# Attention and convolution on one core: the prob x val matmuls of two key chunks together in the odd units

## What is computed

```python
q = q.reshape(B * NUM_HEADS, S, hd)          # likewise k and v; hd = 64
scores = jnp.einsum('gqd,gkd->gqk', q, k) / jnp.sqrt(jnp.asarray(hd, x.dtype))
attn = jax.nn.softmax(scores, axis=-1)
wv = jnp.einsum('gqk,gkd->gqd', attn, v)
...
x = x + _L0_conv_ref(_gn(x), ...)            # _gn: group normalisation, 32 groups
x = x + _L1_conv_ref(_gn(x), ...)            # mask, relu, 3x3 convolution, bias
```

## Time and profile before

| | us |
|---|---|
| runs | 3023.82, 3025.37, 3029.92 |
| median | 3025.37 |
| span of the profiled execution | 3023.4 |
| TensorE busy | 2859.1 (95%) |
| VectorE busy | 2052.7 (68%) |
| ScalarE busy | 1035.4 (34%) |
| GpSimd busy | 897.1 (30%) |
| weigh matmuls (line 535), busy | 545.7 |
| mean granted TensorE clock | 0.983 |

### The profile page before, as it was taken

One profiled execution on the slowest core, in us unless ns is written; L12 is line 12 of the kernel. 1 busy time (PEld: TensorE's weight loads), 2 busy tenths in 40 slices (PEclk: granted clock), 3 DMA queues, 4 the chain that ended last, 5 costly groups with the idle time before them and its releaser, 6 DMA issues.

```text
span 3023.4 us, 41433 instructions
## 1 busy us (share of the span) xinstructions
PE 2859.1 (95%) x12480; PEld 1074.3 (36%) x12480; DVE 2052.7 (68%) x3010; ACT 1035.4 (34%) x1613; POOL 897.1 (30%) x619
## 2 busy tenths in 40 slices
PE   5999999999999999999999999778999999999999
PEld 2333333333333333333333333223444444444444
DVE  6786787687777777768778678987765554654521
ACT  3444444444435434434444344432121121111200
POOL 2343443443434433434343435441110010110100
PEclk9999999999999999999999999989999999999999
DMA  4303313212132142140231231121100101001000
GB/s 131 85 15 78 89 29 81 71 47 78 30 88 60 33 106 57 33 106 24 66 89 33 78 85 32 67 77 56 56 21 35 56 0 55 21 35 56 0 28 28
DMA packets 119928, 167.30 MB, mean 55 GB/s; under 512 B 27296, under 2 KB 76576, under 8 KB 119712
## 3 DMA queue, kind: packets, MB, share of 16 engines
q1 hardware_dynamic: 119712, 164.74, 19.2%
HBM read 80.16 MB, written 33.82 MB: 38 GB/s over the span
## 4 chain that ended last, share of the span: by engine, by line
PE 76%; DVE 11%; issue 5%; DMA 4%; SPq 2%; ACT 1%; DVEq 0%; POOL 0%; ACTq 0%; POOLq 0%
PE bank L625 30%; PE bank L535 11%; PE bank L523 11%; PE bank L480 10%; PE bank L498 6%; PE bank L490 4%; DVE nmax L920 2%; DVE prob_sum L914 2%; DMA den_col<-den_sb 2%; PE bank L512 2%; SPq L337 1%; DVE xn_lo L899 1%; DMA q_b<-shift 1%; DVE filt L962 1%; PE bank L506 1%
## 5 line engine op out<-in xcount | busy, mean ns | idle before, releaser
L625 PE MATMUL bank<-v_hi,filt 128*128 128x512 f16 x3072 | 920.4, 380 | 16.8 <-DVE v_lo L1178 8.7
L674 ACT ACTIVATE prob<-bank 128x512 f32<-128x512 f32 x1024 | 554.9, 593 | 818.5 <-PE bank L523 786.5
L920 DVE TENSOR_REDUCE nmax<-bank 128x1 f32<-128x512 f32 x1024 | 659.0, 682 | 188.7 <-PE bank L498 181.3
L807 POOL TENSOR_TENSOR prob_sum<-prob_sum,prob 128x512 f32<-128x512 f32 x384 | 519.7, 1353 | 730.7 <-ACT prob L674 730.2
L625 PE MATMUL bank<-v_lo,filt 128*128 128x512 f16 x1536 | 584.7, 381 | 0.0
L535 PE MATMUL bank<-prob,val 128*64 128x512 f32 x2048 | 545.7, 621 | 2.1 <-ACT prob L674 2.1
L625 PEld LDWEIGHTS bank<-v_hi,filt 128*128 128x128 f16 x3072 | 302.8, 99 | 383.4 <-issue 23.0
L498 PE MATMUL bank<-k_a,q_a 128*128 128x512 f16 x1024 | 397.6, 389 | 26.0 <-DVE nmax L920 19.7
L914 DVE TENSOR_TENSOR prob_sum<-prob_sum,prob 128x512 f32<-128x512 f32 x384 | 369.1, 961 | 20.9 <-DVE shift L930 19.6
L480 PE MATMUL bank<-mix_mem,w_mem 128*128 128x512 f16 x1024 | 331.7, 387 | 19.4 <-DVE xn_lo L899 19.4
L523 PE MATMUL bank<-q_a,k_a 128*128 128x512 f16 x1024 | 311.1, 385 | 20.6 <-ACT prob L674 20.6
(11 more groups left out here) (97 smaller groups left out, 2468.5 us busy)
## 6 DMA issues: line engine op xcount, KB each, us to landing
xr<-x SPq DMA_DIRECT2D x16, 1024.0 KB, 8.6
k_a<-pad_mem SPq DMA_DIRECT2D x64, 256.0 KB, 5.3
q_a<-pad_mem SPq DMA_DIRECT2D x64, 256.0 KB, 4.8
den_sb<-recip_scratch SPq DMA_DIRECT2D x128, 128.0 KB, 2.8
x_scratch<-xr SPq DMA_DIRECT2D x16, 1024.0 KB, 4.7
xs<-x SPq DMA_DIRECT2D x7, 2048.0 KB, 13.0
k_b<-pad_mem SPq DMA_DIRECT2D x32, 256.0 KB, 5.4
q_b<-pad_mem SPq DMA_DIRECT2D x32, 256.0 KB, 4.9
```

Of the source, the lines that this page charges most:

```text
L625: mm = pe.matmul(bank[co][:].rearrange("p (h w) -> p h w", w=PAIR), u[:, pos, ky, c, co * P:(co + 1) * P], v[:, pos, c, ky:ky + HW, :], st ...
L674: act.activation(prob[:, (2 * u + e) % 8], sc_bank[bank_turn(s * 16 + 2 * u + e, 16 * HPI)[0]][:], ACT.Exp, scale=float(D) ** -0.5).then_i ...
L807: nc.gpsimd.tensor_tensor(acc, in0, prob[:, (2 * kc + 1) % 8], ALU.add).then_inc(s1["sum1"], 1)
L920: dve.tensor_reduce(nmax[:, m // 2, m % 2:m % 2 + 1], src[:], AX.X, ALU.max, negate=True)\
```

## The change

TensorE calls `weigh` for two chunks at a time, in the odd units alone: unit 3 weighs chunks 0 and 1, unit 5 chunks 2 and 3, unit 7 chunks 4 and 5, and unit 1 of the next slot chunks 6 and 7. The matmuls, their operands and the order of the chunks are the same. In unit 1 the denominator's matmuls, which stand in place d, are directly ahead of the pair. ScalarE's copy of pv_bank moves from the end of unit 0 to unit 1, behind its two exps and ahead of that unit's q/k copies.

```diff
+            def weigh_pair(h, s, n):
+
+                weigh(h, s, 2 * n)
+                weigh(h, s, 2 * n + 1)
+
...
-                    if u == 0 and prev:
-                        weigh(h - 1, (s - 1) % HPI, SEG - 1)
-                    if u == 2:
-                        weigh(h, s, 0)
-                    if u >= 2:
-                        weigh(h, s, u - 1)
+                    if u == 1 and prev:
+                        weigh_pair(h - 1, (s - 1) % HPI, SEG // 2 - 1)
+                    if u >= 3 and u % 2:
+                        weigh_pair(h, s, u // 2 - 1)
...
-            weigh(B * HPI - 1, HPI - 1, SEG - 1)
+            weigh_pair(B * HPI - 1, HPI - 1, SEG // 2 - 1)
...
-                    if u == 0 and prev:
+                    if u == 1 and prev:
                         evacuate_pv(h - 1)
```

## The result

The changed kernel takes **3072.96 us** (median of four runs, 3070.17 to 3079.02), the kernel before 3024.6 us beside it (3018.17 to 3029.92). The ratio is 1.0163, with a 95% interval from 1.0145 to 1.0182: it is slower by 48 us. The forecast was 3030 us, 3010 to 3044.

The account below looks back on a forecast made before the run. TensorE bounds four of eight slots, VectorE partly slots 3, 4 and 7, something else slot 1. Switching saved against added waits and a later load sums to +0.7 us an image, +5 us: 3030 us, range 3010 to 3044.

Parts of the forecast that it names:

- The groups and their price: Weigh groups fall from eight to four a slot, each costing 0.24 us of switching: 0.97 us a slot saved.
- three sized waits: PE's added waits: shift matmul for nmin 0.30 us, unit 0 to 1 for an exp 0.30, unit 3 behind ScalarE's copy 0.50.
- without: Slot 5 without the later denominators' load: +0.15 us, against +0.85 with it.
- the later load is paid in full: Slot 5: the denominators' load starts 0.86 us later, PE has no slack, so the slot pays 0.86 us.
- neither moves, and everything that PE saves up to unit 5 is absorbed: Slot 1: the x load and ScalarE's 4.87 us gap stay put, so savings ahead vanish; slot total +0.1 us.
- slot 6: -0.97 + 0.30 + 0.30: Slot 6: switching saved less waits for the first exp and at the shift matmul, -0.35 us.
- slot 7, VectorE again: 0: Slot 7 follows VectorE's pace, so the change brings no difference there: 0 us.
- the hand-made replay: Slot 3 replayed with lighter units: nmin comes some 0.6 us sooner, between -0.5 and +1.0.
- VectorE's stretches "-0.15": Slots 2 and 3: +0.4 us up to slot 3's shift row, -0.6 behind it, -0.15 in all.
- The rival on the other side: Denominators' load later in slot 1 too and no gain in VectorE's stretches: +2.0 us an image, 3041 us; chance 0.29.

Follow-up runs that it names:

- reciprocal late: VectorE's reciprocal of the denominators in unit 5 instead of 3, GpSimd's division in unit 7 instead of 6: changed kernel 2991.9 us, kernel before 2964.1 us.
- halved reductions: Reciprocal in unit 5 and VectorE's max reductions reading 256 of 512 columns: changed kernel 2925.9 us, kernel before 2913.8 us.
- even pairs: Changed kernel with the pairs in units 0, 2, 4, 6 and the denominator alone in unit 1: 2998.2 us, ratio 0.9927 to the kernel before.

## Why the prediction was wrong

**The groups and their price: right.** The pair goes by in 1.87 us (721.90 to 723.77 in the changed kernel's slot 4), as forecast. PE's busy time doesn't show the saving: it falls by 1.9 us in the image where 8 x 0.97 is 7.8, since it has the slower matmuls of slots 1 and 4 in it and short waits vanish under the modelled ends. The starts show it. With the reciprocal late in both kernels, slot 5 has only the three sized waits and no later load, and it differs by +0.14 us; the forecast had +0.15 for it "without".

**The three sized waits: right in size.** In slots 0, 4 and 5 they stand at 0.29 us (exp of unit 0), 0.48 (scores of unit 3) and 0.29 (shift matmul), forecast 0.30, 0.50, 0.30, and L506 follows the last max after 1.38 us. Slot 0 came out at +0.14 by +0.15, slot 5 at +0.99 by +0.85; there the forecast's rule, that the later load is paid in full, held (PE waits 1.0 us for VectorE's bank behind it).

**Failed: slot 1, "neither moves, and everything that PE saves up to unit 5 is absorbed".** Both moved. SP issues the load of x 0.83 us later in the slot (5.32 us by 4.49), since GpSimd's residual add and SP's store, which stand ahead of it, come later by as much. ScalarE's jump back to the start of the loop stands 4.05 us into the slot in both kernels. ScalarE's jump, its next instruction and SP's load of x, before:

```profile
L758 ACTq COMPARE_BRANCH  x1: 45/45/45, 587.2 to 587.2; - x1
L758 ACTq FUSED_REGOPS  x1: 68/68/68, 593.0 to 593.0; - x1
...
587.62 0.40 SPq L372 DMA_DIRECT2D xs<-x  x1
```

and after:

```profile
L761 ACTq COMPARE_BRANCH  x1: 45/45/45, 602.2 to 602.2; - x1
L761 ACTq FUSED_REGOPS  x1: 68/68/68, 604.6 to 604.6; - x1
...
603.44 0.40 SPq L372 DMA_DIRECT2D xs<-x  x1
```

Before, the 2 MB load is issued 0.44 us behind the jump and ScalarE goes on after 5.8 us; in the changed kernel it is issued 1.27 us behind it and ScalarE goes on after 2.45 us. So ScalarE's gap is gone, PE is ready for its first max of unit 5 23.8 us into the slot instead of 28.35, and stands 4.8 us behind a load that lands when it did (the reciprocal 27.8 us into the slot, 27.5 before). I looked for what the saving *ahead* of a wait would be absorbed by, and not for whether the wait itself would stay, nor for what the next wait behind it would cost; and the clock fell there. The loss is 2.6 us an image where 0.1 was forecast. The step that failed is thus the premise that the x load and ScalarE's gap stay where they are. The pair's own saving and small waits were right in this slot too.

**Failed: "slot 6: -0.97 + 0.30 + 0.30", and "slot 7, VectorE again: 0".** The working asked at each emptied unit which ScalarE or VectorE result is just behind PE for the scores and the shift matmul. It did not ask it for the max matmuls, whose banks VectorE frees 0.68 us apart. That PE never idles in slots 5 and 6 says that VectorE keeps up *with the weigh groups between the max matmuls*. Three max matmuls come in each of units 2 to 4, 2 us of VectorE's work plus an add; a single chunk in every unit spreads them out, a pair in every other unit bunches them. Slot 6 adds up in PE's starts: 0.57 us (the first exp, forecast 0.30), 0.56 ahead of the value projection of unit 3 (L490, VectorE's bank, not in the forecast), 0.30 and 0.54 at the two banks (not in the forecast), 0.28 at the shift matmul (forecast 0.30), less 0.97, make +1.28; measured +1.27. In slot 7 one wait of 1.0 us became two of 0.9, and an exp (0.7) and the shift matmul (1.5) come late as well; in slot 3 the reductions end later instead of 0.6 us sooner, as the hand-made replay had it.

**Failed by sign: VectorE's stretches "-0.15".** Slots 2 and 3 came to +1.4. Late, slot 3 of the changed kernel is still 1.4 us longer than that of the kernel before, and with halved reductions the two are alike (23.70 and 23.75 us): it is VectorE's pace. Which reduction starts the delay I haven't isolated. The clock may have a part: it falls in slot 3 in three of the loop's images after the change and in two before, and these slots take 1.4 to 3.0 us more than the others.

**The rival on the other side** (3041 us, the load later everywhere) named the right load, but not what happened to it: in slot 1 the load lands only 0.3 us later (mean of six images), and PE comes 4.5 us earlier. The range stopped at 3044 since no term in it could be larger than a microsecond a slot. Taken away one behind the other, the causes are 20.6 us (late reciprocal: the load in the changed kernel, ScalarE's gap in the one before), 15.7 (VectorE) and 17.3 (the copy ahead of ScalarE's queue, moved in the changed kernel alone), and 5.2 remain as a gain: 48.4. Each figure holds in this order only, give or take some 6 us; the copy gave 6, 9 and 17 us by the medians of its three runs and 10, 13 and 13 by their loop means.

**Why ScalarE's gap comes and goes.** The traces order it cleanly. Fourteen kernels have six jumps each with a load of x beside it. Where SP issues that load 0.7 us ahead of the jump or 0.5 behind it (the kernel before and the one with even pairs), ScalarE goes on 3.7 to 6.8 us behind the jump. Where it is issued 1.2 us behind the jump or later (the twelve others, 72 jumps), ScalarE goes on after 2.4 to 3.4 us. Between jump and next instruction there are packets of a queue that the profile calls instruction (q14, 8 KB each). In the images above they lie between 591 and 592 us before and between 603.0 and 603.4 after (queue, kind: packets, MB, share):

```profile
q14 instruction: 2, 0.02, 4.1%
```

```profile
q14 instruction: 1, 0.01, 5.7%
```

The last of them starts 4.0 us behind the jump in the kernel before and 0.9 to 1.3 us behind it in the changed one, in both 1.5 to 2.4 us ahead of that instruction. So ScalarE's next instructions seem to stand behind the bytes of x. That is argued from the order of times in these 84 jumps: the profile doesn't say whose instructions the packets hold, and no run moved the load of x alone.

## What to carry to other kernels

An instruction group that costs its engine 0.24 us of switching may be the time in which another engine catches up; before groups are merged, list at every place that becomes empty each bank that the next matmuls need, the reduction's banks too, and when its reader ends. When a working says that a wait or a transfer "doesn't move", follow what it stands behind, engine by engine: 0.83 us at a load of x decided here whether ScalarE stood still for 5 us. And before a gain is put down to the wait that an edit removes, list what else the edit moves. The late reciprocal gave 60 us of 3024, more than the whole change under test moved, and most of what slot 1 gained by it was not the wait it was meant for. And an edit that gains on one kernel (the even pairs, 25 us) may gain next to nothing on another; the same edit with the suspected wait gone tells it.

## What the runs showed of the hardware that was not expected

An idle stretch of TensorE cost more than its length. In slot 1 of the changed kernel, 4.8 us of waiting is followed by projections 0.43 us apart instead of 0.216 (the lower level), 0.95 of granted clock for the slot. With the late reciprocal neither kernel has it (1.00): the edit returned 6.5 us in that slot of the changed kernel's image shown, where the wait measured 4.8.

Slot 4 has it too, in all seven images of the loop in the changed kernel (0.94 or 0.95) and in three of seven before. It begins behind the wait for nmin at the end of slot 3:

```profile
695.13 0.39 PE L506 MATMUL bank<-cst,nmin 128*8 128x128 f32 x2 [3.12 <-DVE nmin L927]
...
697.18 2.81 PE L535 MATMUL bank<-prob,val 128*64 128x512 f32 x8
```

The pair takes 2.74 us to the next max matmul (699.92) instead of 1.87. A lower clock need not cost anything: before, slot 4 takes 29.83 or 29.84 us in six of the loop's images, with a granted clock of 1.00 in three of them and of 0.94 in three.

ScalarE's jump at the end of its loop took 2.4 us to its next instruction at best where a load of x was beside it, and up to 6.8 us where 2 MB were issued from 0.7 us ahead of it to 0.5 us behind it. The gap stands in the profile as "issue", and nothing in the list of waits names the transfer.
